# A state-space, FFN and recurrent-attention block on one core: a ring of twelve scan tiles and four sets of replicated rows, with all orders written anew

## The reference

```python
x = x + attn_a(layernorm(x))     # selective state-space layer, 512 channels x 16 states
x = x + ffn(layernorm(x))        # silu(gate) * up, 768 hidden, int8-valued weights
x = x + attn_b(layernorm(x))     # recurrent attention, 1024 channels
x = x + ffn(layernorm(x))        # the same FFN again
```

```python
dt = softplus(einsum(dt, W_dt) + b_dt)
A_bar = exp(dt[..., None] * A)                       # the decay, A = -exp(A_log)
Bu = dt[..., None] * Bm[:, :, None, :] * xc[..., None]
_, h_all = associative_scan(comb, (A_bar, Bu), axis=1)   # h[t] = A_bar[t] h[t-1] + Bu[t]
y = einsum('bldn,bln->bld', h_all, Cm) + D_param * xc
y = y * silu(z)
```

## Time and profile before

| | us |
|---|---|
| median of 3 runs | 1663.07 (1662.47 to 1665.38) |
| the profiled execution | 1667.68 |
| its span, first to last instruction | 1665.9 |
| VectorE busy | 1467.1 (88%) |
| TensorE busy | 1518.8 (91%) |
| GpSimd busy | 1313.8 (79%) |
| ScalarE busy | 1211.1 (73%) |

### The profile page before, as it was taken

One profiled execution on the slowest core, in us unless ns is written; L12 is line 12 of the kernel. 1 busy time (PEld: TensorE's weight loads), 2 busy tenths in 40 slices (PEclk: granted clock), 3 DMA queues, 4 the chain that ended last, 5 costly groups with the idle time before them and its releaser, 6 DMA issues. The chain is left out here.

```text
span 1665.9 us, 19103 instructions
## 1 busy us (share of the span) xinstructions
PE 1518.8 (91%) x5026; PEld 748.9 (45%) x5026; DVE 1467.1 (88%) x1997; ACT 1211.1 (73%) x1993; POOL 1313.8 (79%) x693
## 2 busy tenths in 40 slices
PE   6886899879999998999899998999899999999978
PEld 2321344344544553364434463354544553546454
DVE  3898989899989899999999999899999999975761
ACT  5656688858788678869788778988697778555621
POOL 0478997999699987999799997999689998842430
PEclk9898899999999999999999999999999999999988
DMA  7563444443446134463346334453355523312211
GB/s 228 186 202 124 158 150 134 129 151 102 137 153 230 41 128 160 129 207 120 126 159 213 121 119 158 152 183 114 106 155 170 178 88 126 100 57 62 74 45 32
DMA packets 163519, 225.22 MB, mean 135 GB/s; under 512 B 13458, under 2 KB 104083, under 8 KB 163411
## 3 DMA queue, kind: packets, MB, share of 16 engines
q1 hardware_dynamic: 163410, 223.99, 41.1%
HBM read 179.90 MB, written 39.85 MB: 132 GB/s over the span
## 5 line engine op out<-in xcount | busy, mean ns | idle before, releaser
L921 POOL TENSOR_TENSOR bu<-rep,bc 128x1024 f32<-128x1024 f32 x256 | 600.4, 2363 | 140.2 <-PE ps_y L1449 65.9
L1085 ACT ACTIVATE ps_d<-rep,scale_a 128x512 f32<-128x512 f32 x512 | 338.4, 684 | 155.1 <-DVE bu L1262 101.1
L1385 PE MATMUL ps_r<-xT,wgu 128*128 128x512 f32 x768 | 351.3, 603 | 7.8 <-ACT xT L1093 2.2
L1255 DVE TENSOR_TENSOR_SCAN ps_d<-ps_d,bu 128x512 f32<-128x512 f32 x272 | 322.6, 1214 | 11.9 <-ACT ps_d L1085 8.3
L927 POOL TENSOR_TENSOR bu<-bu,bc 128x1024 f32<-128x1024 f32 x120 | 282.9, 2363 | 20.1 <-DVE bu L1255 18.9
L1255 DVE TENSOR_TENSOR_SCAN bu<-ps_d,bu 128x512 f32<-128x512 f32 x240 | 285.3, 1209 | 15.0 <-POOL bu L921 10.3
L1385 PE MATMUL ps_r<-mix,wkv 128*128 128x512 f32 x512 | 247.9, 616 | 26.9 <-ACT kv L1122 12.6
L962 ACT ACT_TABLE_LOAD x191 | 245.1, 1283 | 3.4
L1385 PEld LDWEIGHTS ps_r<-xT,wgu 128*128 128x128 f32 x768 | 141.5, 191 | 210.2 <-issue 197.8
L940 POOL TENSOR_TENSOR kv<-sums,kv 128x1024 f32<-128x1024 f32 x64 | 150.7, 2354 | 46.3 <-DVE sums L1352 45.7
L1262 DVE TENSOR_TENSOR bu<-ps_d,bc 128x512 f32<-128x512 f32 x272 | 178.2, 678 | 1.0
(11 more groups left out here) (112 smaller groups left out, 2105.8 us busy)
## 6 DMA issues: line engine op xcount, KB each, us to landing
rep<-dd_scratch SPq DMA_DIRECT2D x128, 512.0 KB, 5.1
wgu<-gu_scratch SPq DMA_DIRECT2D x96, 256.0 KB, 3.6
dd_scratch<-dd SPq DMA_DIRECT2D x32, 512.0 KB, 4.2
bc<-bc_scratch SPq DMA_DIRECT2D x64, 256.0 KB, 4.1
wr<-w_r_dram SPq DMA_DIRECT2D x64, 128.0 KB, 3.4
xc_scratch<-xc SPq DMA_DIRECT2D x32, 256.0 KB, 4.4
sz_scratch<-xin SPq DMA_DIRECT2D x32, 256.0 KB, 3.6
wo<-w_o_dram SPq DMA_DIRECT2D x16, 512.0 KB, 4.5
```

The source lines that it names most:

```text
L921: pool.tensor_tensor(bu[:, i % BU:i % BU + 2, :], rep[:, g % REP:g % REP + 2, 1, :], bc[:, 0, q, :].unsqueeze(1).to_broadcast([P, 2, T]), ...
L1085: act.activation(ps_d[D_BANK[i]][:, :], rep[:, g % REP, 0, :], ACT.Exp, scale=scale_a[:, a, NQ * j + q:NQ * j + q + 1]).then_inc(decay_rea ...
L1255: dve.tensor_tensor_scan(states, d[:, :], bu[:, i % BU, :], 0.0, ALU.mult, ALU.add)\
L1385: last = pe.matmul(dst, lhs, rhs, start=n == 0, stop=n == len(pairs) - 1)
```

## The change

The ring holds 12 tiles in place of 8, and `rep` holds 4 sets in place of 6; four more tiles of 2 KB per partition take the room of two sets of 4 KB. As 64 steps do not divide by 12, a tile's slot is counted through all sequences. `g_bu` of step i now waits for the sum of step i - 12. With 4 sets, no set of the next block can be loaded until the block's own four last tiles have released theirs; that now holds at all 31 changes of block, not at the 7 where a sequence starts.

```diff
-DB, BU, REP, RB, WS, EU, WI, WF = 3, 8, 6, 4, 3, 3, 2, 3
+DB, BU, REP, RB, WS, EU, WI, WF = 3, 12, 4, 4, 3, 3, 2, 3
...
+def tile_slot(s, i):
+
+    return (STEPS * s + i) % BU
...
-                        pool.tensor_tensor(bu[:, i % BU:i % BU + 2, :], rep[:, g % REP:g % REP + 2, 1, :],
+                        pool.tensor_tensor(bu[:, tile_slot(s, i):tile_slot(s, i) + 2, :], rep[:, g % REP:g % REP + 2, 1, :],
...
-                        states = bu[:, i % BU, :] if by_pool(s, i) else d[:, :]
-                        dve.tensor_tensor_scan(states, d[:, :], bu[:, i % BU, :], 0.0, ALU.mult, ALU.add)\
+                        states = bu[:, tile_slot(s, i), :] if by_pool(s, i) else d[:, :]
+                        dve.tensor_tensor_scan(states, d[:, :], bu[:, tile_slot(s, i), :], 0.0, ALU.mult, ALU.add)\
...
-                            last = pe.matmul(ps_y[CH * a:CH * (a + 1), :], sel[:, :], bu[:, (NA * i + a) % BU, :],
+                            last = pe.matmul(ps_y[CH * a:CH * (a + 1), :], sel[:, :], bu[:, tile_slot(s, NA * i + a), :],
```

(The two slots of `g_hc` and the one of `v_hc` change in the same way.) The tables are replaced whole; one line of each kind:

```diff
-        "g_bu*4 g_hc g_bu*3 g_hc g_bu*5 g_hc g_bu*4 g_hc g_bu*3 g_hc g_bu*3 g_hc g_bu*2 g_dt g_bu*4 g_hc g_dt "
+        "g_bu*4 g_hc g_bu*4 g_hc g_bu*3 g_hc g_bu*5 g_hc g_bu*3 g_hc g_bu*5 g_hc g_dt g_bu g_dt g_bu*4 g_hc "
```

More of the change, by code:

```diff
@@ new lines @@
+        "hp_turn*2 p_in*4 p_warm p_in*3 p_xproj p_in p_dt*4 p_warm*35 p_y p_warm*2 hp_turn*2 p_in*2 p_y p_in*2 "
+        "p_y p_warm*3 p_y p_in*4 p_y p_warm p_y p_warm*5 p_y p_warm*10 p_y p_xproj p_y p_dt*3 p_y p_dt p_y "
+        "p_warm*8 p_y*3 hp_turn p_warm*6 p_y hp_turn p_warm*3 p_y p_post*2 p_y p_warm*3 p_y fp_turn fp_turn2 "
+        "fp_turn fp_turn2 p_warm fp_gate fp_up p_warm p_y fp_gate fp_up p_y fp_gate fp_up p_y p_warm fp_gate "
+        "fp_up fp_gate fp_up fp_gate p_y fp_up p_in fp_down fp_down2 fp_down p_y*2 fp_down2 p_in*2 p_y p_warm "
@@ new lines @@
+        "p_in p_warm fp_turn p_warm fp_turn2 p_in p_y fp_turn fp_turn2 p_in*2 p_xproj p_in p_dt p_k p_y "
+        "p_recept*2 p_y p_k p_v p_k p_dt p_v p_recept*2 p_y p_recept*3 p_dt p_recept p_v p_warm*8 p_k p_y p_v "
+        "p_dt p_y p_k p_warm*5 p_k p_v p_y p_v hp_turn p_k p_post p_wo p_wo2 p_y p_post p_wo p_wo2 p_v fp_turn "
+        "fp_turn2 p_k p_y*2 fp_turn fp_turn2 fp_gate fp_up fp_gate fp_up p_y fp_gate fp_up fp_gate fp_up fp_gate "
+        "fp_up p_v fp_gate fp_up p_y hp_turn fp_down fp_down2 fp_down fp_down2 p_in*2 p_y p_wo p_wo2 fp_turn p_y "
@@ new lines @@
+        "fp_up p_v p_y fp_gate fp_up hp_turn fp_down fp_down2 fp_down fp_down2 p_y hp_turn p_wo p_wo2 p_wo "
+        "fp_turn fp_turn2 fp_turn fp_turn2 p_wo2 p_in*2 p_y p_k p_in*2 rp_turn rp_turn2 p_y rp_turn rp_turn2 "
+        "p_in*2 p_v p_k p_in p_y p_in p_xproj p_dt p_y p_recept*3 p_v p_k p_dt p_recept p_v p_y*2 rp_gate rp_up "
+        "rp_gate rp_up p_k p_recept p_v p_y rp_gate rp_up p_recept rp_gate rp_up rp_gate rp_up p_y p_recept "
+        "rp_gate rp_up p_k p_v p_y rp_down rp_down2 rp_down rp_down2 p_recept p_k p_y*2 p_v p_wo p_wo2 p_post*2 "
@@ new lines @@
+        "p_recept p_dt p_v p_y rp_gate rp_up*2 rp_gate p_y rp_up p_y p_recept*2 p_k rp_down rp_down2 p_y rp_down "
+        "rp_down2 p_post p_k p_post p_recept p_y*2 p_v p_wo p_wo2 p_v fp_turn p_y fp_turn2 fp_turn fp_turn2 "
+        "fp_gate fp_up fp_gate p_k fp_up p_v p_y fp_gate fp_up fp_gate p_wo p_wo2 fp_up p_y fp_gate fp_up fp_gate "
+        "p_k fp_up p_y p_v fp_down p_dt fp_down2 p_dt fp_down fp_down2 p_y p_wo p_wo2 p_wo p_y p_wo2 fp_turn "
+        "fp_turn2 fp_turn fp_turn2 hp_turn*2 p_in p_k p_in rp_turn rp_turn2 p_v p_in rp_turn rp_turn2 p_in "
@@ L1261, in run @@
                         dve.wait_ge(scanned.sem, at(scanned, s, i + 1))
-                        dve.tensor_tensor(bu[:, i % BU, :], ps_d[D_BANK[i]][:, :], bc[:, 1, q, :], ALU.mult)\
+                        dve.tensor_tensor(bu[:, tile_slot(s, i), :], ps_d[D_BANK[i]][:, :], bc[:, 1, q, :], ALU.mult)\
                             .then_inc(hc_ready.sem, 1)
```

488 lines of the change are left out of this document (235 added, 253 removed), and 117 rows, old and new, of tables (BANKS, ORDER).

## The result

The changed kernel takes 1670.22 us (median of 12 runs, 1665.86 to 1676.70) against 1662.87 us of the kernel before, timed beside it: ratio 1.0047, 95% interval [1.0034, 1.0061]. It is slower by 7.4 us, where 5.5 us less was forecast. A second timing gave 1.0051 [1.0033, 1.0069]. The profiled execution took 1673.1 us, with a span of 1671.3, so the two traces differ by 5.4 us. The twelve executions lie up to 11 us apart, so the ratios decide and the traces tell only where.

What follows compares the result with a forecast made beforehand. VectorE was taken to bound the long scan stretch (94.6% busy, 75.5 us idle) and TensorE the tail. Terms -10 + 3 + 0 + 1.5 + 0 = -5.5 us from 1663.1 gave 1657.6, say 1658; own range 1645 to 1668, 8 in 10 1638 to 1684.

Steps and rivals of the forecast that it cites:

- The start: Up to the sixth scan: loads go out near 47.9 us, sixth scan 1.5 us earlier or 1.2 later; taken as 0.
- The ring of 12: GpSimd's waits for sums ahead of B products: sums may come one group later, 10 us gained, bounds 0 and 21.7.
- Four sets: Changes of block: first scans wait for late loads of rows, 3 us lost, ends 0 and 10.0.
- The queue behind it: SP's list: FFN and attention weights listed behind a waiting `rep` load come later, but are prefetched; costed at nothing.
- The rest of the orders: VectorE's other 40 us of idle time, drawn anew: taken as 0, with 8 to 20 us either way.
- Table loads, tail and fillers: ScalarE's eight more table loads cost 1.5 us; tail 0, with 3 us either way; six fewer fillers on TensorE 0.
- GpSimd's 65.9 us: Sign: GpSimd's idle time ahead of B products until TensorE's sums are done should fall by more than half.
- VectorE's idle time: Sign in the scan stretch, 75.5 us before: the forecast is wrong if it is above 80 us.
- Decays waited for rows: Sign on ScalarE: the forecast is wrong if decays wait for rows for more than 20 us.
- GpSimd's 7.0 us for rows: Sign: GpSimd's wait for replicated rows ahead of B products should rise to 20 us or more.
- The scans' waits: Sign: VectorE's waits for products should fall from 13.8 to about 4 us plus some 3 at changes of block.
- The rival in which four sets bind: First decay and product behind every change of block: loads of rows come late, about 1686 us; chance 0.17.

Runs made afterwards that it cites:

- run 1: The changed kernel with the start of the kernel before (orders up to about the sixth scan): 1.0023 times before.
- run 4: The kernel before with the start of the changed kernel, up to the sixth scan: 1.0068 times before.
- Run 5: The changed kernel with GpSimd's first product held until the step-size products of all four blocks of the first sequence are made: 1.0015 times before.
- Run 8: The kernel before under its own orders, with four sets of rows, a fitted SyncE list and a ring of twelve tiles: 1.0248 times before.
- run 7: The kernel before under its own orders and ring of eight, with four sets of rows and SyncE's list fitted to them: 1.0259 times before.
- Run 9: The kernel before with its six sets and ring of eight, but the SyncE list that was fitted to four sets: 1.0070 times before.
- run 13: The changed kernel with 26 late loads of rows moved ahead in SyncE's list: 1.0029 times before.
- run 2: The changed kernel with the tail of the kernel before (orders of about the last 220 us): 1.0072 times before.
- run 3: The changed kernel with both the start and the tail of the kernel before: 1.0046 times before.
- run 10: The kernel before with GpSimd's first product held until the first three blocks' step-size products are made: 0.9986 times before.
- run 14: The changed kernel with late loads of rows moved ahead in SyncE's list and GpSimd's first product held for all four blocks' step sizes: 0.9998 times before.
- run 16: The kernel before with GpSimd's first product held for three blocks' step sizes, timed again on another chip job: 0.9968 times before.

## Why the prediction was wrong

Two steps failed. The start was put at 0 and costs time, by VectorE instructions that wait for GpSimd's products. And the four sets were put at +3 beside a ring worth -10, as if the two were independent: by the waits in the traces the ring's gain came, and the rows took it back. This second half is read from the waits; no run isolates it. In the two traces the sixth scan is 5.9 us late and everything behind it takes as long as before, 1596.3 us for 1596.8.

*The start, put at 0: wrong, it costs 4 us by run 1 and 11 by run 4.* The step saw the right rows and the right mechanism and stopped one instruction short. It let the loads go out near 47.9; they went at 50.19, because the second store came at 48.52 and not 46.4. The missing table load was eaten up ahead of it: TensorE's product of `xc` and `wx` starts at 30.71 instead of 28.12, the first block's step sizes start on VectorE at 41.15 instead of 37.80, and the second block's at 45.55, where before it was 45.48. The first units of ScalarE and VectorE stand in a new order there; which of them does it wasn't tried. First product 57.78 for 56.2. Then the fourth block's work was placed at 54.8 to 57.7 and met one product at its end; in fact it began at 57.42, just ahead of the first product. Each of its next three instructions waited for one of GpSimd's products, 3 x 2.0 us. The forecast bounded the first scan by 61.4; it was 66.3. Run 5 takes that overlap away and nothing else, and is 5.3 us shorter, of which 2.2 are there at the sixth scan.

The Trainium skill (SBUF — State Buffer, section SBUF: two separate sides) says that the port pair goes to whoever starts first, for a whole instruction, and lists as contenders on VectorE only those in a two-port mode or with two inputs in SBUF. The traces agree: 0.69 becomes 2.7 us for the instructions with two SBUF inputs, while the scans (1.2 us) and the products with a PSUM input (0.69) beside the same products of GpSimd don't change. The rule as the forecast used it was right; that it strikes each instruction of a chain anew was not worked out.

*The ring of 12, put at -10: the mechanism held, the sum lost it.* GpSimd's wait for the sums fell by 70%, and what sums cost the scans fell from 9.5 to 0.5 us, close to the 10 of the forecast. That it doesn't show in the time is the next step's doing. Run 8 against run 7 gives 1.8 us, but both have four sets, and there too the rows come last once the sums don't. No run has the ring of twelve with six sets, so what it is worth alone is open.

*Four sets, put at +3 with 0 and 10.0 as ends: mis-sized.* What rows cost the scans rose from 3.7 to 11.8 us, 8.1 more, which is the ring's gain again. The reading of the earlier trace rows was wrong here: the 14.9 us "for nothing that the view shows" were waits for rows too, so rows already cost GpSimd 21.9 us and not 7.0. And the 3 us were taken from the seven starts of sequences, where the order was written by hand for such loads. Under before's orders, with their list of loads, the sets cost +31 us and the list +12. The measure compared a release with the next scan and let VectorE's other work absorb the rest. It left out that a decay or product that waits holds up everything behind it in its engine's list: there 13.4 of the 43 us are waits of scans, two thirds are waits for other things.

*The queue behind it, put at 0: wrong.* Run 9's 12 us are places in SyncE's list, and so are run 13's 3 us as far as overlapping intervals tell, though not by the path considered: not weights late behind rows, but rows late behind weights.

*The rest of the orders, put at 0 with 20 us either way: wrong.* Under twelve and four, the new orders are 1.0047 against 1.0248, 33 us better, start included; 12 of the 33 may be the list of loads that was made for run 7. The forecast took the change's parts as independent. They are not: the orders pay for the missing sets. 43 - 2 - 33 = 8 us is the measured sum. That the new orders run with less waiting for rows than run 8 (69.6 us for 107.6) is shown; which of their moves does it wasn't tried.

*Table loads, tail and fillers, +1.5, 0, 0.* 199 loads at 1283 ns with 3.6 us of idle, as foretold; their effect was not isolated. In the stretch from 1450 to 1666 us TensorE works 200.7 us for 198.7, but the kernel goes on until 1671.3: the tail is 5.3 us longer than the 216 of the forecast, and counted from the last sums 3.0. Runs 2 and 3 don't show that its order makes this.

Of the signs named, GpSimd's 65.9 us, the table loads and VectorE's idle time came out as said. Decays waited for rows 8.9 us, below the limit of 20. GpSimd's 7.0 us for rows rose to 13.1 under that name, short of the 20 that were said, and to 60.7 with "issue". The scans' waits, the time of the loads, the tail and the first scan did not come out, and the first scan at 66.3 us was the one to look at first. The rival in which four sets bind was priced with a slip, 1663 + 26 being 1689 and not 1686; nothing hangs on it.

## What to carry to other kernels

Where two engines share a port, lay the whole dependent chain beside the other engine's list and charge every instruction of it; where the chain gates the next stage, let the other engine start later. A wait that the profile gives no name to still has an owner: read in the code what the instruction waits for, and lay the landings of loads beside it, before calling it free. When two waits meet at one instruction, removing the one that ends last is worth only the distance to the other. The cost of fewer buffers is not the lateness of the next consumer: an in-order engine that waits for a buffer delays all that stands behind it, and the size of it is only known with the orders that go with it. A load into a scarce buffer belongs at the place in the queue where the buffer comes free, ahead of loads that wait for something else.

## What the runs showed of the hardware

Beside GpSimd's 128x1024 products a VectorE instruction with two SBUF inputs of 128x512 took 2.7 to 2.9 us for 0.69, one for each product of GpSimd, in 16 of the 20 traces; in the four without it (runs 5, 10, 14 and 16) the first product was held. Holding GpSimd back by some 2 us in the kernel before made it 2 to 5 us shorter. Two executions of the same start put the first scan at 66.3 and 67.4 us, and the same lists with another tail at 69.0, so a trace of one execution can't carry an argument about 2 us.
